# One product for q, k and v per token tile, keys normalised before the transpose, biases inside shifted weights

## The chip, the core and the metric

The kernel runs on one core of a Trainium2 chip. The metric is the device time of a run in microseconds (us). Of the kernel before there are three runs; their median is 128.02 us, the lowest 126.82 us, the highest 130.88 us. TensorE (PE), VectorE (DVE), ScalarE (ACT) and GpSimd (POOL) each work through a queue of their own in order; the DMAs here are issued on the queues of SyncE (SP) and ACT.

## The reference, cut to what matters

The input x is 4 batches of 512 tokens with 128 channels. A context of 4 x 77 tokens with 96 channels comes with a mask. Two blocks are computed, each added to its input:

```
ln = layernorm(layernorm(x)) * gl + bl        # latents, 128 channels
xn = layernorm(ctx) * gx + bx                 # context, 96 channels
q  = ln @ Wq.T;  k, v = [xn @ Wkv.T ; ln @ Wlkv.T]      # 77 + 512 keys, 2 heads of 64
qn = rmsnorm(q) * gq / 8;  kn = rmsnorm(k) * gk          # per head
out = softmax(qn @ kn.T, masked context keys) @ v
x  = x + out @ Wo.T + bo
h  = layernorm(x);  gates = softmax(h @ Wg + bg)          # 8 experts
x  = x + sum over the 2 largest gates of  gate * (h @ W[e] + b[e])
```

All eight expert products are computed for every token, and the gates that are not chosen are zero.

## The kernel before

Tokens are handled in tiles of 128 (T = 4 per batch, 16 in all). `FRONT` lists the units of the first part (batch 0 in two units of two tiles, the others whole), `REAR` those of the rest (batch 3 in two halves). Four strings, `TENSOR` (L27), `VECTOR` (L48), `SCALAR` (L61) and `GPSIMD` (L72), write out by hand in which order each engine issues its jobs; each word names a function of that engine, a unit and an index. In `TENSOR` the last word of a job names its PSUM banks, and `free` (L937) makes PE wait until the bank's former user has been read. Between engines all is ordered by semaphores.

The front of a unit: DVE takes the statistics (`stats1`), POOL the inverse root with a power (`rstd1`), DVE normalises (`apply1`), PE transposes (`xT`, L985), ACT applies gain and bias (`lnT`, L513). PE then makes q token-major (`q`, L994: lnT loaded, 128 columns of Wq streamed), v likewise (`v`, L1012), and k channel-major (`k`, L1003: the weight loaded, up to 512 tokens streamed). q is squared (ACT), summed (DVE `ssq`), raised to -0.5 (POOL `rq`, L395), multiplied (DVE `qn`) and transposed (`qT`). k is squared on ACT and summed over channels by small products with `heads` (`ssk`, L1022); its inverse root `rk` (POOL, L401) is not applied to k: it is the scale of the exponential (L588), whose partitions are the keys. Queries and keys are each split into a rounded part and a rest (`QH`, `QL`, `KH`, `KL`), and a score is three products of float32r parts (L1077).

The attention: for each batch and each of 5 blocks of keys (4 of 128 tokens, 1 of 77 context tokens) PE makes the scores of both heads, ACT takes one exponential per head, PE multiplies with v (`value`, L1098). For the denominators POOL adds key blocks 0+1 and 2+3 (`e01` L420, `e23` L429), DVE adds the two sums and the context block (`esum1` L796, `esum2` L803), and PE sums over partitions (`den`, L1111), followed by a transpose (`denT`), the output projection (`proj`, L1132) and the sum with x (`xbo`, `x2`).

The experts: second normalisation (`stats2`, `rstd2`, `apply2` L843), transpose (`l2T`, L1141), two copies on ACT and a rest on POOL (`l2L`, L457), gate logits token-major (`gate`, L1150: 32 loads of tokens with 8 columns each), the two best gates (`logits`, `top`), a transpose of split gates and one product with a block matrix of biases (`w3`, `gateT`, `wT`, `bias` L1167, `x2b`). For each tile experts 0 to 3 (`low`) and 4 to 7 (`high`) are each three products of 512 columns (L945 to L947). ACT scales the four low experts (L635), POOL adds them (`pair` L470, L471), DVE adds the high ones in a chain (`high`, L923, for two tiles at a time), POOL makes the last sum (`res`, L479), and SP stores. In `TENSOR` four `high` blocks of batch 0 stand among the scores of batches 2 and 3, and one `low` block in batch 3's.

## Time and profile before

| what | value |
|---|---|
| median of 3 runs | 128.02 us (126.82 to 130.88) |
| profiled execution: span from first to last instruction | 123.7 us |
| profiled execution's own time beside its span | not listed apart; the median run is 4.3 us over the span, the lowest 3.1 us |
| mean granted TensorE clock | 0.958 of full |
| PE busy (matmuls) | 106.9 us, 86% |
| DVE busy | 97.5 us, 79% |
| POOL busy | 91.0 us, 74% |
| ACT busy | 76.6 us, 62% |
| last instruction's end to the end of the span | 121.6 to 123.7 us: the last store |

The span is the time between the first and the last instruction of one profiled execution. Busy time is a sum over the whole span. The ends of matmuls are modelled, since they are pipelined; what one costs in a full queue is read from the distance between two starts. A group such as "x8" holds eight instructions of one kind in a row. A product of plain float32 operands shows as two instructions, one of float32r operands as one.

### The profile page before, as it was taken

The page shows a single profiled execution, that of the slowest core. Times are in us where ns is not written, and L with a number is a line of the kernel's source. Part 1 is how long each engine was busy: PE and PEld are TensorE (multiplying, and loading weights), DVE is VectorE, ACT ScalarE, POOL GpSimd, SP SyncE. Part 2 cuts the span into 40 slices and gives each one's busy share as a digit, 9 for nine tenths or more (in the row PEclk, how much of TensorE's full clock was granted, in tenths as well). Part 3 has the DMA queues.
Part 4 walks back from the last instruction along what each step waited for, and adds up shares of the span by engine and source line. Part 5 has one row for each costly group of instructions (what it writes and reads, how often), then busy time and mean ns, then how long its engine had stood idle before and what let it go on. Part 6 is the DMA issues. An engine that isn't in the chain of part 4 may idle for free. (4 is left out here: it accounts for less than half of the span.)

```text
span 123.7 us, 2493 instructions
## 1 busy us (share of the span) xinstructions
PE 106.9 (86%) x683; PEld 69.0 (56%) x683; DVE 97.5 (79%) x376; ACT 76.6 (62%) x177; POOL 91.0 (74%) x117
## 2 busy tenths in 40 slices
...
GB/s 122 119 22 130 168 169 0 5 0 0 0 3 0 5 0 0 0 0 5 0 5 0 0 0 5 0 0 5 0 42 3 3 42 42 38 10 42 42 42 42
DMA packets 5971, 3.44 MB, mean 28 GB/s; under 512 B 2407, under 2 KB 5575, under 8 KB 5959
## 3 DMA queue, kind: packets, MB, share of 16 engines
...
q10 hardware_dynamic: 832, 0.36, 1.1%
...
q14 instruction: 6, 0.05, 0.1%
HBM read 2.24 MB, written 1.05 MB: 27 GB/s over the span
## 5 line engine op out<-in xcount | busy, mean ns | idle before, releaser
L588 ACT ACTIVATE probs<-PS,shift,rk 128x512 f32<-128x512 f32 (+1 forms) x40 | 25.5, 691 | 9.6 <-PE PS L1077 9.3
L635 ACT ACTIVATE scaled<-PS,w 128x128 f32<-128x128 f32 x64 | 18.4, 375 | 9.7 <-PE PS L947 7.0
L1098 PE MATMUL PS<-probs,V_sb 128*64 128x512 f32 (+1 forms) x80 | 18.2, 532 | 0.0
L420 POOL TENSOR_TENSOR esum<-probs,probs 128x1024 f32<-128x1024 f32 (+1 forms) x5 | 10.7, 2147 | 7.2 <-ACT probs L588 7.2
L945 PE MATMUL PS<-WeH,l2H 128*128 128x512 f32 x32 | 14.3, 446 | 0.5 <-ACT scaled L635 0.5
L470 POOL TENSOR_TENSOR pair<-scaled 128x256 f32<-128x256 f32 x16 | 12.0, 751 | 2.8 <-ACT scaled L635 1.5
L946 PE MATMUL PS<-WeL,l2H 128*128 128x512 f32 x32 | 13.3, 414 | 0.0
L947 PE MATMUL PS<-WeH,l2L 128*128 128x512 f32 x32 | 13.1, 410 | 0.0
L429 POOL TENSOR_TENSOR e<-probs,probs 128x1024 f32<-128x1024 f32 (+1 forms) x5 | 9.7, 1936 | 2.6 <-ACT probs L588 2.6
L1077 PE MATMUL PS<-QH,KH 64*128 64x512 f32 (+1 forms) x40 | 9.5, 463 | 0.4 <-DVE QL L766 0.4
L719 DVE TENSOR_SCALAR xh<-x_sb,mv,rstd 128x128 f32<-128x128 f32 x16 | 8.1, 566 | 2.0 <-POOL rstd L388 2.0
L923 DVE SCALAR_TENSOR_TENSOR part<-PS,w,part 128x128 f32<-128x128 f32 x32 | 8.9, 340 | 0.0
L1077 PEld LDWEIGHTS PS<-QH,KH 64*128 64x128 f32 x40 | 4.2, 198 | 8.4 <-issue 7.2
L843 DVE TENSOR_SCALAR l<-x,mv,rstd 128x128 f32<-128x128 f32 x16 | 7.8, 542 | 1.1 <-POOL rstd L448 1.1
L471 POOL TENSOR_TENSOR low<-pair 128x128 f32<-128x128 f32 x16 | 7.7, 482 | 1.3
L945 PEld LDWEIGHTS PS<-WeH,l2H 128*128 128x128 f32 x32 | 6.4, 200 | 3.2 <-issue 1.1
L479 POOL TENSOR_TENSOR x2b<-low,acc 128x128 f32<-128x128 f32 x16 | 7.3, 462 | 0.9 <-DVE acc L923 0.7
L591 ACT ACTIVATE probs<-PS,cbias,crk 77x512 f32<-77x512 f32 (+1 forms) x10 | 6.4, 686 | 2.6 <-PE PS L1077 1.8
L1077 PE MATMUL PS<-QL,KH 64*128 64x512 f32 (+1 forms) x40 | 7.9, 381 | 0.0
L457 POOL TENSOR_TENSOR l2L<-l2T,l2H 128x512 fp32r<-128x512 f32 (+1 forms) x5 | 5.3, 1059 | 3.3 <-ACT l2H L618 3.3
L1077 PE MATMUL PS<-QH,KL 64*128 64x512 f32 (+1 forms) x40 | 7.8, 375 | 0.0
L401 POOL TENSOR_TENSOR rk<-msk,half 128x8 f32<-128x8 f32 (+1 forms) x5 | 7.1, 1424 | 0.9 <-DVE msk L743 0.9
...
## 6 DMA issues: line engine op xcount, KB each, us to landing
out_dram<-x2b SPq DMA_DIRECT2D x7, 128.0 KB, 1.7
...
x_sb<-in_x_dram SPq DMA_DIRECT2D x2, 128.0 KB, 2.4
bias_raw<-in_L_ffn_b_dram SPq DMA_DIRECT2D x12, 4.0 KB
Wlkv_sb<-in_L_xattn_Wlkv_dram ACTq DMA_DIRECT2D x1, 128.0 KB, 2.8
...
```

The lines of the kernel that those rows point to most:

```text
L420: pool.tensor_tensor(esum[p % 2][:, :, s], probs[p % 2][0][:, :, s], probs[p % 2][1][:, :, s], ALU.add).then_inc(e01_made, 1)
L429: pool.tensor_tensor(e23[:, :, s], probs[p % 2][2][:, :, s], probs[p % 2][3][:, :, s], ALU.add).then_inc(e23_made, 1)
L470: step(pool.tensor_tensor(pair[:], scaled[m % 2][:, 0:EH // 2], scaled[m % 2][:, EH // 2:EH], ALU.add))
L588: act.activation(probs[p % 2][n][:, h, s], ps[:, s], ACT.Exp, bias=shift[:, 0:1], scale=rk[:, b, n, h:h + 1]).then_inc(probs_made, 1)
L635: last = act.activation(scaled[m % 2][:, e], ps[:, e], ACT.Copy, scale=w[:, m, e:e + 1])
L719: last = dve.tensor_scalar(xh[:, b % 2, t], x_sb[:, b, t], mv1[:, b, t, 0:1], rstd1[:, b, t:t + 1], ALU.subtract, ALU.mult)
L923: last = dve.scalar_tensor_tensor(dst, bank("high", p, 2 * n + k)[:, e * C:(e + 1) * C], w[:, m, EH + e:EH + e + 1], src, ALU.mult, ALU.add)
L945: pe.matmul(dst, lH, rH, start=True, stop=False)
L946: pe.matmul(dst, lH, rL, start=False, stop=False)
L947: return pe.matmul(dst, lL, rH, start=False, stop=True)
L1077: last = pe.matmul(bank("score", p, n, h)[0:P if n < T else M, 0:(e - a) * P], k, queries[r, b % 2, a * P:e * P], start=(step == 0), stop= ...
L1098: last = pe.matmul(bank("value", p, 0)[h * D:(h + 1) * D, s], v, pr, start=(n == 0), stop=(n == KT - 1))
```

## The change

All front units have two tiles, the rear units are whole batches. PE makes q, k and v of a tile in one product of 384 columns into two adjacent banks (`qkv`; PSUM is now four tensors of two banks). Keys are treated as queries are: squares, sums, power and product token-major over 256 channels (`sq`, `ssq`, `rq`, `qkn`), then both are transposed (`qkT`) and split (`qkH`, `qkL`). The context is handled alike (`ckv`, `csq`, `ctx_ss`, `ckn`, `ckT`). The exponential has no per-key scale any more and covers both heads in one instruction over two banks. DVE's two sums for the denominators are gone; PE sums three sources instead (`den`). A normalised row sums to zero, so the last channel's weight can be subtracted from all others and the last row and channel used for the bias: expert and gate weights are shifted on POOL (`weS`, `wgS`), channel 127 of `l2` is one, and the bias product with its preparation is gone. The expert weights are split on ACT (`weH`) and POOL (`weL`) rather than on DVE, and loaded after all of x. The gate is computed channel-major: 32 weight columns loaded, 128 tokens streamed, the four tiles in four groups of columns, for both parts of the tokens; ACT copies, and PE transposes. The rest `l2L` moves from POOL to DVE and reads PSUM. POOL's last sums go over two tiles at once. All four orders are written anew; 31 of the 32 expert blocks now stand behind the last `value` (before, 27).

```diff
-FRONT = ((0, 0, 2), (0, 2, 4), (1, 0, 4), (2, 0, 4), (3, 0, 4))
-REAR = ((0, 0, 4), (1, 0, 4), (2, 0, 4), (3, 0, 2), (3, 2, 4))
-
+FRONT = tuple((b, a, a + 2) for b in range(4) for a in (0, 2))
+REAR = ((0, 0, 4), (1, 0, 4), (2, 0, 4), (3, 0, 4))
+JOINED = (0, 1, 2, 3)
...
+    weights 0 0 0   weights2 0 0 1   xT 0 0 0   xT 1 0 2   qkv 0 0 45   ctxT 0 0 0   qkv 1 0 23   xT 3 0 0   ckv 0 0 67
+    qkv 3 0 01   qkT 0 0 4   xT 2 0 5   qkT 1 0 2   maskT 0 0 3   qkv 2 0 45   ckT 0 0 3   score 0 0 67   score 0 1 01
+    score 0 2 23   qkT 3 0 6   value 0 0 7   score 0 3 01   value 0 1 -   score 0 4 23   value 0 2 -   xT 4 0 0
+    xT 7 0 1   value 0 3 -   xT 5 0 1   value 0 4 -   qkT 2 0 0   qkv 4 0 23   qkv 5 0 45   score 1 3 01   xT 6 0 6
+    den 0 0 7   score 1 0 01   proj 0 0 67   score 1 1 23   denT 0 0 0   value 1 0 1   score 1 2 45   value 1 1 -
+    score 1 4 23   value 1 2 -   qkT 5 0 0   value 1 3 -   qkT 4 0 2   value 1 4 -   qkv 6 0 45   score 2 3 01
+    score 2 0 23   den 1 0 6   qkv 7 0 01   score 2 1 67   score 2 2 23   qkT 6 0 4   value 2 0 5   score 2 4 67
+    value 2 1 -   l2T 0 0 4   qkT 7 0 0   proj 1 0 12   value 2 2 -   denT 1 0 3   gate 0 0 0   value 2 3 -
+    score 3 0 67   value 2 4 -   score 3 3 01   den 2 0 4   proj 2 0 52   score 3 1 67   denT 2 0 3   value 3 0 4
+    score 3 2 01   l2T 1 0 6   gateT 0 0 7   value 3 1 -   score 3 4 23   value 3 2 -   gate 1 0 5   value 3 3 -
+    gateT 1 0 5   low 0 3 6   value 3 4 -   den 3 0 7   proj 3 0 01   denT 3 0 7   high 0 0 2   low 0 2 3   high 0 1 6
+    low 0 0 4   low 0 1 5   high 0 2 3   high 0 3 7   l2T 2 0 4   low 1 3 2   low 1 2 5   gate 2 0 4   low 1 1 2
+    gateT 2 0 4   low 1 0 6   high 1 3 3   high 1 1 5   high 1 2 7   high 1 0 6   l2T 3 0 2   low 2 2 4   gate 3 0 7
+    low 2 3 0   low 2 1 1   gateT 3 0 4   low 2 0 7   high 2 1 5   high 2 2 0   high 2 3 6   high 2 0 4   low 3 2 7
...
+    consts 0 0   stats1 0 0   stats1 1 0   ctx_stats 0 0   apply1 0 0   apply1 1 0   gain 0 0   mask 0 0   stats1 3 0
+    ctx_apply 0 0   stats1 2 0   apply1 3 0   ssq 0 0   shift 0 0   ssq 1 0   apply1 2 0   qkn 0 0   ctx_ss 0 0
+    qkn 1 0   ssq 3 0   qkL 0 0   ckn 0 0   cbias 0 0   qkL 1 0   qkn 3 0   ckL 0 0   stats1 6 0   stats1 7 0
+    stats1 4 0   ssq 2 0   stats1 5 0   apply1 7 0   apply1 6 0   apply1 4 0   apply1 5 0   qkn 2 0   qkL 3 0   qkL 2 0
+    ssq 4 0   ssq 5 0   qkn 4 0   qkn 5 0   x2 0 0   qkL 5 0   qkL 4 0   stats2 0 0   ssq 6 0   apply2 0 0   qkn 6 0
+    ssq 7 0   qkL 6 0   qkn 7 0   l2L 0 0   qkL 7 0   x2 1 0   stats2 1 0   apply2 1 0   x2 2 0   logits 0 0   l2L 1 0
+    stats2 2 0   mark 0 0   logits 1 0   top 0 0   mark 1 0   apply2 2 0   top 1 0   x2 3 0   sum 0 0   stats2 3 0
+    l2L 2 0   sum 0 1   logits 2 0   apply2 3 0   mark 2 0   sum 1 1   l2L 3 0   top 2 0   sum 1 0   logits 3 0
+    mark 3 0   top 3 0   sum 2 1   sum 2 0   sum 3 1   sum 3 0
 """
...
+    ident 0 0   rstd1 0 0   blanks 0 0   rstd1 1 0   ctx_rstd 0 0   rstd1 3 0   rstd1 2 0   rq 0 0   rq 1 0   ctx_rk 0 0
+    rq 3 0   xbo 1 0   xbo 0 0   rstd1 6 0   rstd1 7 0   rstd1 4 0   rstd1 5 0   rq 2 0   e01 0 0   e23 0 0   rq 4 0
+    rq 5 0   weS 0 0   e01 1 0   e23 1 0   xbo 2 0   wgS 0 0   rstd2 0 0   rq 6 0   rq 7 0   e01 2 0   e23 2 0
+    rstd2 1 0   weL 0 0   e01 3 0   e23 3 0   rstd2 2 0   xbo 3 0   pair 0 1   pair 0 0   rstd2 3 0   res 0 0   res 0 1
+    pair 1 1   pair 1 0   res 1 1   pair 2 1   res 1 0   pair 2 0   res 2 1   pair 3 1   res 2 0   res 3 1   pair 3 0
+    res 3 0
...
+        PS = [st.enter_context(nc.psum_tensor(f"PS{n}", [P, 2, S], F32)) for n in range(4)]
...
+            sp.wait_ge(Wg_zeroed, 2)
+            sp.dma_start(WgS[P - 1:P, 0:E], row(bg)).then_inc(bg_in, 16)
+            sp.dma_start(We_sb[0:P - 1], We[:, 0:P - 1].rearrange("e h o -> h e o")).then_inc(We_in, 16)
+            sp.dma_start(We_last[:], We[:, P - 1:P].rearrange("e h o -> h e o").to_broadcast([P - 1, E, C])).then_inc(We_in, 16)
+            sp.dma_start(We_sb[P - 1:P], be.rearrange("(a e) o -> a e o", a=1)).then_inc(We_in, 16)
...
+            def weS_(p, n):
+
+                pool.wait_ge(We_in, 48)
+                pool.tensor_tensor(We_sb[0:P - 1], We_sb[0:P - 1], We_last[:], ALU.subtract).then_inc(WeS_made, 1)
+
+            def weL_(p, n):
+
+                pool.wait_ge(WeH_made, 1)
+                pool.tensor_tensor(WeL[:], We_sb[:], WeH[:].bitcast(F32), ALU.subtract).then_inc(WeL_made, 1)
+
+            def wgS_(p, n):
+
+                pool.wait_ge(Wg_in, 32)
+                pool.tensor_tensor(WgS[0:P - 1, 0:E], Wg_sb[:], Wg_last[:], ALU.subtract).then_inc(WgS_made, 1)
+
...
+            def sq_(p, n):
+                b, a, e = FRONT[p]
+                act.wait_ge(qkv_done, after("pe", "qkv", p))
+                if p >= 2:
+                    act.wait_ge(ssq_made, after("dve", "ssq", p - 2))
+                act.activation(qksq[:, p % 2], both("qkv", p, 0)[:, :, 0:2 * C], ACT.Square).then_inc(qksq_made, 1)
+
+            def v_(p, n):
+                b, a, e = FRONT[p]
+                act.wait_ge(qkv_done, after("pe", "qkv", p))
...
+            def qkH_(p, n):
+
+                b, a, e = FRONT[p]
+                act.wait_ge(qkT_done, after("pe", "qkT", p))
                 act.wait_ge(gain_made, 1)
...
+                    act.wait_ge(scores_done, after_all("pe", "score", [(b - 2, k) for k in range(KT)]))
+                act.activation(QH[:, b % 2, a * P:e * P], bank("qkT", p, 0)[:, 0:(e - a) * P], ACT.Copy, scale=gain[:, 0:1])
+                act.copy(KH[:, b % 2, a * P:e * P], bank("qkT", p, 0)[:, (e - a) * P:2 * (e - a) * P]).then_inc(qkH_made, 1)
...
+                ps = both("score", p, n)
+                    act.activation(probs[p % 2][n][:], ps[:], ACT.Exp, bias=shift[:, 0:1], scale=1.0).then_inc(probs_made, 1)
+                    act.activation(probs[p % 2][n][0:M], ps[0:M], ACT.Exp, bias=cbias[:, p:p + 1],
+                                   scale=1.0).then_inc(probs_made, 1)
...
+            def gs_(p, n):
+                b, a, e = REAR[p]
+                act.wait_ge(gate_done, after("pe", "gate", p))
+                act.copy(gsb[0:(e - a) * GW, p], bank("gate", p, 0)[0:(e - a) * GW, 0:P]).then_inc(gs_made, 1)
...
+            def qkn_(p, n):
+                b, a, e = FRONT[p]
+                dve.wait_ge(rqk_made, after("pool", "rq", p))
+                dve.wait_ge(v_made, after("act", "v", p))
+                if p >= 2:
+                    dve.wait_ge(qkT_done, after("pe", "qkT", p - 2))
+                dve.tensor_tensor(qkn[:, p % 2].rearrange("p t (g d) -> p t g d", d=D),
+                                  both("qkv", p, 0)[:, :, 0:2 * C].rearrange("p t (g d) -> p t g d", d=D),
+                                  rqk[:, b, a:e].unsqueeze(3).to_broadcast([P, e - a, 2 * H, D]),
+                                  ALU.mult).then_inc(qkn_made, 1)
...
+                dve.wait_ge(qkH_made, after("act", "qkH", p))
...
+                dve.scalar_tensor_tensor(QL[:, b % 2, a * P:e * P], bank("qkT", p, 0)[:, 0:g], gain[:, 0:1],
+                                         QH[:, b % 2, a * P:e * P].bitcast(F32), ALU.mult, ALU.subtract)
+                dve.tensor_tensor(KL[:, b % 2, a * P:e * P], bank("qkT", p, 0)[:, g:2 * g],
+                                  KH[:, b % 2, a * P:e * P].bitcast(F32), ALU.subtract).then_inc(qkL_made, 1)
...
-            def esum1_(p, n):
-
-                s = slice(0, (REAR[p][2] - REAR[p][1]) * P)
-                dve.wait_ge(e01_made, p + 1)
-                dve.wait_ge(e23_made, p + 1)
-                step(dve.tensor_tensor(esum[p % 2][:, :, s], esum[p % 2][:, :, s], e23[:, :, s], ALU.add))
-
-            def esum2_(p, n):
-
-                s = slice(0, (REAR[p][2] - REAR[p][1]) * P)
-                dve.wait_ge(dve_step, count[0])
-                dve.wait_ge(probs_made, H * KT * (p + 1))
-                dve.tensor_tensor(esum[p % 2][0:M, :, s], esum[p % 2][0:M, :, s], probs[p % 2][T][0:M, :, s],
-                                  ALU.add).then_inc(esum_made, 1)
...
+                    last = dve.tensor_scalar(l2[:, b % 2, t, 0:C - 1], x2[:, b, t, 0:C - 1], mv2[:, b, t, 0:1],
+                                             rstd2[:, b, t:t + 1], ALU.subtract, ALU.mult)
...
+            def l2L_(p, n):
+                b, a, e = REAR[p]
+                dve.wait_ge(l2H_made, after("act", "l2H", p))
+                dve.tensor_tensor(l2L[:, b % 2, a * P:e * P], bank("l2T", p, 0)[:, 0:(e - a) * P],
+                                  l2H[:, b % 2, a * P:e * P].bitcast(F32), ALU.subtract).then_inc(l2L_made, 1)
...
+                    last = pe.matmul(both("qkv", p, 0)[:, t - a, 0:3 * C], lnT[:, b % 2, t * P:(t + 1) * P], WT[:],
+                                     start=True, stop=True)
+                last.then_inc(qkv_done, 1)
...
+            def qkT_(p, n):
+                b, a, e = FRONT[p]
+                free("qkT", p, 0)
+                pe.wait_ge(qkn_made, after("dve", "qkn", p))
+                for s in range(2):
+                    for t in range(a, e):
+                        k = s * (e - a) + t - a
+                        last = pe.transpose(bank("qkT", p, 0)[:, k * P:(k + 1) * P], qkn[:, p % 2, t - a, s * C:(s + 1) * C], ident[:])
+                last.then_inc(qkT_done, 1)
...
+                sources = [(e01[k], P), (e23, P), (probs[k][T], M)] if p in JOINED else \
+                    [(e01[k], P), (probs[k][2], P), (probs[k][3], P), (probs[k][T], M)]
+                pe.wait_ge(e01_made, after("pool", "e01", p))
+                if p in JOINED:
+                    pe.wait_ge(e23_made, after("pool", "e23", p))
+                pe.wait_ge(probs_made, after_all("act", "exp", [(p, i) for i in range(KT)]))
+                for i, (src, rows) in enumerate(sources):
+                    for h in range(H):
+                        for g in range(2):
+                            r = slice((2 * h + g) * 32, (2 * h + g + 1) * 32)
+                            last = pe.matmul(bank("den", p, 0)[r, 0:c], ones[0:rows], src[0:rows, h, g * c:(g + 1) * c],
+                                             start=(i == 0), stop=(i == len(sources) - 1))
                 last.then_inc(den_done, 1)
...
+                pe.wait_ge(bg_in, 16)
+                for i, tokens in enumerate((l2H, l2L)):
+                    for t in range(a, e):
+                        last = pe.matmul(bank("gate", p, 0)[(t - a) * GW:(t - a + 1) * GW, 0:P], WgS[:],
+                                         tokens[:, b % 2, t * P:(t + 1) * P].bitcast(F32), start=(i == 0), stop=(i == 1))
```

## Rows read from the trace of the kernel before

**Rows 1.** Windows; columns: PE, PEld, DVE, ACT, POOL busy (count); PEclk; DMA; GB/s.

```profile
17.50:86.60 69.10, 68.66 (x488) 39.32 (x488) 57.71 (x189) 47.92 (x86) 50.14 (x39) 0.98 0.01 2
86.60:123.70 37.10, 27.33 (x133) 20.83 (x131) 29.31 (x136) 20.21 (x71) 30.65 (x55) 0.91 0.09 29
```

**Rows 2.** Timeline of PE, 46 to 57 us: start, duration, what.

```profile
46.59 1.02 PE L1003 MATMUL PS<-lnT,WT 128*128 128x512 f32 x2
...
50.41 0.50 PE L1077 MATMUL PS<-QH,KH 64*128 64x512 f32 x2
...
51.31 1.08 PE L1098 MATMUL PS<-probs,V_sb 128*64 128x512 f32 x4
52.31 1.05 PE L1022 MATMUL PS<-heads,ksq 128*128 128x2 f32 x8
53.23 0.63 PE L1141 MATMUL PS<-ident,l 128*128 128x128 f32 x4
...
54.80 0.64 PE L1111 MATMUL PS<-esum,ones 128*32 128x256 f32 x8
55.37 1.06 PE L1150 MATMUL PS<-Wg_sb,l2T 128*128 128x8 f32 x8
56.28 0.41 PE L1120 MATMUL PS<-ident,den_sb 128*128 128x128 f32 x2
```

**Rows 3.** Timeline of PE at 256 columns, and the last value product.

```profile
78.15 0.39 PE L1077 MATMUL PS<-QH,KH 64*128 64x256 f32 x2
...
78.69 0.65 PE L1098 MATMUL PS<-probs,V_sb 128*64 128x256 f32 x4
...
86.04 0.65 PE L1098 MATMUL PS<-probs,cV 77*64 77x256 f32 x4
```

**Rows 4.** Timeline of PE in the tail: two expert blocks of three products.

```profile
91.68 0.39 PE L945 MATMUL PS<-WeH,l2H 128*128 128x512 f32 x1
...
92.38 0.40 PE L945 MATMUL PS<-WeH,l2H 128*128 128x512 f32 x1
```

**Rows 5.** Timeline of the head, all engines.

```profile
10.94 0.58 ACT L513 ACTIVATE lnT<-PS,ln_cols 128x256 f32<-128x256 f32 x1
...
17.52 0.61 PE L1077 MATMUL PS<-QH,KH 64*128 64x512 f32 x2 [0.36 <-DVE QL L766]
```

**Rows 6.** Groups with shapes kept apart: the power and the exponential.

```profile
L588 ACT ACTIVATE probs<-PS,shift,rk 128x512 f32<-128x512 f32 x24 | 17.3, 776 | 7.6 <-PE PS L1077 7.5
...
L588 ACT ACTIVATE probs<-PS,shift,rk 128x256 f32<-128x256 f32 x16 | 8.2, 565 | 2.0 <-PE PS L1077 1.7
...
L395 POOL TENSOR_TENSOR rq<-msq,half 128x8 f32<-128x8 f32 x3 | 5.0, 1660 | 0.2
```

**Rows 7.** Windows of 2 us where the granted clock fell, columns as rows 1.

```profile
18.00:20.00 2.00, 2.00 (x12) 1.84 (x10) 1.97 (x13) 0.95 (x2) 2.00 (x3) 0.50 0.00 1
...
110.00:112.00 2.00, 2.00 (x6) 1.52 (x6) 1.90 (x14) 0.22 (x1) 1.75 (x4) 0.50 0.00 0
```

**Rows 8.** Groups by line: out<-in xcount, busy, mean ns, idle before.

```profile
L923 DVE SCALAR_TENSOR_TENSOR part<-PS,w,part 128x128 f32<-128x128 f32 x32 | 8.9, 340 | 0.0
...
L401 POOL TENSOR_TENSOR rk<-msk,half 128x8 f32<-128x8 f32 (+1 forms) x5 | 7.1, 1424 | 0.9 <-DVE msk L743 0.9
...
L796 DVE TENSOR_TENSOR esum<-esum,e 128x1024 f32<-128x1024 f32 (+1 forms) x5 | 6.0, 1193 | 0.9 <-POOL e L429 0.9
L803 DVE TENSOR_TENSOR esum<-esum,probs 77x1024 f32<-77x1024 f32 (+1 forms) x5 | 5.4, 1083 | 0.0
```

**Rows 9.** Timeline of POOL in the tail.

```profile
112.32 0.73 POOL L470 TENSOR_TENSOR pair<-scaled 128x256 f32<-128x256 f32 x1 [0.17 <-POOL x2b L479]
...
114.18 0.75 POOL L470 TENSOR_TENSOR pair<-scaled 128x256 f32<-128x256 f32 x1 [0.17 <-POOL x2b L479]
```

**Rows 10.** Timeline of DVE: the second normalisation, twice.

```profile
51.20 1.12 DVE L843 TENSOR_SCALAR l<-x,mv,rstd 128x128 f32<-128x128 f32 x4 [0.91 <-POOL rstd L448]
...
65.45 2.71 DVE L843 TENSOR_SCALAR l<-x,mv,rstd 128x128 f32<-128x128 f32 x4
```

More of the change, by code:

```diff
@@ L484, in _ @@
+            for kind, p, n in JOBS["pool"]:
+                does[kind](p, n)
         @block.scalar
@@ new lines, in dens_, with oT_ @@
+            def dens_(p, n):
+                act.wait_ge(den_done, after("pe", "den", p))
+                if p >= 2:
+                    act.wait_ge(denT_done, after("pe", "denT", p - 2))
+                act.copy(den_sb[:, p % 2], bank("den", p, 0)[:, 0:S // 2]).then_inc(dens_made, 1)
+            def oT_(p, n):
+                act.wait_ge(values_done, after("pe", "value", p, KT - 1))
+                if p >= 2:
+                    act.wait_ge(proj_done, after_all("pe", "proj", rears(p - 2)))
+                act.copy(oT[:, p % 2], bank("value", p, 0)[:]).then_inc(oT_made, 1)
@@ L641, in _ @@
+            for kind, p, n in JOBS["act"]:
+                does[kind](p, n)
         @block.vector
@@ L817, in x2_ @@
+                dve.wait_ge(denT_done, after("pe", "denT", b))
+                c = T // 2
+                sums = bank("denT", b, 0)[:, 0:c * P].rearrange("p (c h g k) -> p c h g k", c=c, h=H, g=2)
+                for g in range(a // c, e // c):
+                    divided = step(dve.reciprocal(rden[:, b, g * c:(g + 1) * c], sums[:, :, :, g, 0]))
+                dve.wait_ge(proj_done, after("pe", "proj", p))
                 dve.wait_ge(dve_step, divided)
@@ new lines, in sum_ @@
+                        if e < EH - 1:
+                            summed[i] = step(last)
+                last.then_inc(acc_made, 1)
+            does = dict(consts=consts_, gain=gain_, shift=shift_, mask=mask_, cbias=cbias_, stats1=stats1_,
+                        apply1=apply1_, ssq=ssq_, qkn=qkn_, qkL=qkL_, ctx_stats=ctx_stats_, ctx_apply=ctx_apply_, ctx_ss=ctx_ss_,
+                        ckn=ckn_, ckL=ckL_, x2=x2_, stats2=stats2_, apply2=apply2_, l2L=l2L_, logits=logits_, mark=mark_,
+                        top=top_, sum=sum_)
@@ L935, in _ @@
+            for kind, p, n in JOBS["dve"]:
+                does[kind](p, n)
         @block.tensor
@@ L1146, in gate_ @@
                 free("gate", p, 0)
[L1147 to L1151 removed]
+                pe.wait_ge(l2L_made, after("dve", "l2L", p))
+                pe.wait_ge(WgS_made, 1)
+                pe.wait_ge(Wg_zeroed, 2)
+                pe.wait_ge(bg_in, 16)
```

868 lines of the change are left out of this document (319 added, 549 removed).

## The prediction

> **What bounds the kernel now.** I read the totals on the page first: PE 86%, DVE 79%, POOL 74% and ACT 62% busy. No engine is full over the whole span, so I cut the span where its limit changes, and asked for each engine's busy time in each piece. The cuts are the first score at 17.5 us [rows 5] and the end of the last product of probabilities with values [rows 3]. That gives a head of 17.5 us, an attention part of 69.1 us and a tail of 37.1 us, 123.7 in all.
>
> In the attention part PE is busy 68.7 of 69.1 us, DVE 57.7, POOL 50.1, ACT 47.9 [rows 1]. The reader is to see that only PE has no room: a microsecond taken from another engine there is worth nothing by itself. In the tail PE has 27.3 of 37.1 us, DVE 29.3 and POOL 30.7 [rows 1], and 2.5 us at the very end are the last store with what goes before it. There POOL works tile after tile at 1.86 us [rows 9], and DVE is nearly as full. The head is a chain of single steps, each waiting for the one before: from the second unit's `lnT` to the first score it takes 6.6 us [rows 5].
>
> PE's costs I take from the distance between two starts in the full stretch [rows 2], since busy times of pipelined products overlap. Where a group's successor is not shown I take its busy time less 0.07 us, by which the value product's 1.08 exceeds its distance of 1.00.
>
> **The head: +2.5 us.** In the chain to the first score, k now goes every way that q goes. The product is 384 columns wide where q was 128: two products of 512 columns take 0.95 us [rows 2], so 4 x 256 added columns take 0.95. The power on POOL is 128x8 and takes 1.66 us [rows 6]; the narrow form is (7.1 - 3 x 1.66) / 2 = 1.06 [rows 6, 8], so +0.6. Square, sum, product, rounding and rest are each 256 elements wider, and by the exponential's 0.72 against 0.51 us of busy time each such step costs 0.2 [rows 6]: +1.0. Sum 2.55. Against it, PE makes `xT` of both units before any product, and for it, `ctx_stats` now stands ahead of `apply1` on DVE. Bounds: 0 (a chain that runs wholly inside waits that are there already) to +4.5 (each of the two units pays most of it, since POOL's powers queue). I take 2.5.
>
> **The attention part: -6.5 us**, all on PE.
> - `xT` and `qkv` of batch 1 move into the head, where PE has holes: four transposes 0.56, and 8 x 384 columns at 0.475 per 512, 2.85 [rows 2]. Together -3.4. What hides them is PE's wait for the first keys; without that cover they come back in full.
> - q, k and v stream as many columns as before, 3 x 1,024 per batch: 0 (at best -0.3 for fewer switches).
> - `ssk` goes, 0.92 per batch [rows 2], batches 1 to 3: -2.8. The transposes of k come, 0.56 each: +1.7.
> - The denominators have three sources: 0.57 becomes 1.71 [rows 2] in three batches: +3.4. This is the price of DVE's sums, 6.0 + 5.4 us [rows 8], which lay beside PE's work. `den` now waits for POOL's `e23` itself. The worst place is batch 3, where `proj` and nearly all experts are queued behind `den` on PE; between the exponential that `e23` needs and `den` lie three value products, a score, a gate and an expert block, over 5 us, against POOL's one sum.
> - The gate: 0.91 us now [rows 2]. Sixteen products of 128 columns in four column groups cost 0.57 if they run as `den` does (eight of 256 columns, 0.57), and 1.8 if the groups do not overlap at 0.11 each. The former is the nearer row, also in four groups: -0.3 in two batches, -0.6.
> - Batch 3 is no longer halved: ten scores at 0.54 and ten values at 0.58 [rows 3] become five at 0.90 and five at 1.00 [rows 2]: 11.2 - 9.5, -1.7.
> - Expert blocks in this part fall from 5 to 1, 0.70 each [rows 4]: -2.8, which the tail takes over. One bias product: -0.25.
>
> The sum is -6.45. ACT's gain, 16 x 2 exponentials into 16, is several us, but ACT was idle 21 us here; 0. POOL loses `rk`, 7.1 us [rows 8], and `l2L`, and gets eight wide powers and two passes over the expert weights; it stays far under PE. SP's queue issues fewer DMAs (twelve small bias loads go), and x comes before the expert weights. Those, with a spread copy of their last row about twice the bytes, are first waited for by POOL behind its sixth `rq`, well inside this part; queued there is `e01` of batch 1, on which only its `den` waits: 0.
>
> **The tail: -2 us.** PE: 31 blocks at 0.70 are 21.7; `den` 1.7, `proj` and `denT` 1.2, two `l2T` 1.1, two gates with transposes 1.5, so 27.2. After the last block come DVE's sums of two tiles, 8 x 0.28 = 2.2 [rows 8], POOL's last sum and the store, 3.6: 33.0 if PE sets the pace. POOL per two tiles needed 3.72 [rows 9]; wider instructions bring it between 1.86 (only fixed cost) and 3.72 (none), I take the middle near 2.9, 23 for eight, and `l2L` is off it. So POOL stops being the limit. DVE is next: it must wait for the third part of `x2`, about 5.6 us into the tail, then do eight pairs, 17.8, and second statistics, normalisation, `l2L`, two or three rounds of gates, about 8: 31.4, and 3.6 to the end, 35. DVE sets the end, at 35 against 37.1. Bounds: 33 and 38.
>
> **Sum.** +2.5 - 6.5 - 2 = -6, so the span goes from 123.7 to 117.7. The median of the runs shown is 4.3 us over the span; I carry that along: 128.0 - 6 = **122 us**.
>
> **Rivals.** A difference of 2% is about what a measurement of this kernel can tell from none: 125.5 and 130.6 us are the marks.
> - *Nothing is waited for more, and the clock stays up.* The granted clock was 0.50, that is 1.2 GHz, in 18 to 20 us, after PE had waited in the head, and again in 110 to 112, after holes in the tail [rows 7]; each window lost 1 us. If the head stays at 17.5 and half of these losses go, and DVE keeps up with PE in the tail: 122 - 2.5 - 2 - 1 = 116.5. For: all four engines get less work. Against: the longer chain. Chance 0.18.
> - *The saving is waited away at both ends.* The head at its upper bound (+2) and DVE at 37 in the tail (+2): 126. For: DVE's order mixes sums with gates, and the `high` banks are freed only by them. Chance 0.17.
> - *POOL's longer instructions hold DVE.* The second normalisation takes 1.12 us alone, but 2.71 when POOL is inside a sum [rows 10]. In the tail it stands twice beside POOL sums twice as wide as now: 2 x 1.6, 125.2. Chance 0.06. [...]
> - *Slower: each batch starts with a wait.* The first score of a batch now needs the keys and queries of both its units, by `after_all`, and the chain before it is 6.6 + 2.5 us long. In batches 1 to 3 PE has work for it only if the hand-written orders place the units early enough on four engines. If PE waits 2.5 us at each and then works 2 us at half clock, as after the head [rows 7], that is 2.5 + 1 in each, 10.5 in all: 132.5. It decides from 2.9 us a batch (8.6 to the mark). For: there are eight powers of 1.66 on POOL. Against: DVE and POOL had 11 and 19 us to spare in the attention part. Chance 0.13. The Trainium skill, "TensorE: Matmul & The Clock Gate", section "What's actually happening", says that the slow clock is the default and activity releases it; that speaks against a change that takes work off PE and lengthens its first wait.
>
> My forecast has 0.46. Faster by over 2%: 0.46 + 0.18 + 0.05 of the lock's 0.06 = 0.69. Within 2%: 0.17 + 0.01 = 0.18. Slower: 0.13. The range runs from 115 (the best case and 1.5 us of its unknowns) to 129 (the second rival and 3 us); the last rival is left out, and a little at the lower end.
>
> **What would show it.** First score near 20 us. The part from there to the last value product near 62.5 us with PE busy throughout; each `den` near 1.7 us between starts, a `qkv` unit near 1.4, a gate near 0.6. In the tail DVE the fullest engine and POOL at 3 us or less per two tiles. I am wrong if PE has holes ahead of the first score of batches 1 to 3, if `den` waits for POOL, or if POOL still sets the end.

## Result: 11% slower, and the profile after

The changed kernel takes 141.65 us (median of 4 runs, 141.38 to 141.81) beside 128.06 us for the kernel before (126.82 to 130.88) on the same chip: a ratio of 1.114, 95% interval 1.105 to 1.123. The forecast was 122, range 115 to 129. The profiled run took 141.38 us with a span of 139.6, so 1.8 us lie around a span. The runs of one kernel fall into two groups (the kernel before near 126 and near 131); every ratio here compares lower group with lower group, so it isn't the quotient of the medians, and below I give the median of a kernel's lower group beside that of all its runs, as "lower median".

Page of the changed kernel: the span in 40 slices, 3.5 us each.

```profile
span 139.6 us, 2250 instructions
...
PE   0587987999999995000089999999999996799940
...
PEclk9999999999999999755558999999999999559999
DMA  4354000000000000000000000000000020101121
GB/s 133 80 123 143 17 22 24 22 27 22 24 22 22 27 22 22 22 21 2 0 0 0 0 5 0 0 2 0 5 0 0 5 78 0 38 2 38 38 75 38
```

Two things are new. PE, which had no hole in this part before [rows 1], stands empty in slices 17 to 20. And a transfer runs at 22 GB/s for fourteen slices, from about 14 to 63 us, where none ran before: the attention part had 2 GB/s [rows 1]. The same as windows; columns are those of rows 1:

```profile
14.00:34.00 20.00, 18.72 (x96) 9.80 (x94) 14.77 (x48) 13.72 (x26) 17.18 (x20) 1.00 0.08 22
...
70.00:80.00 10.00, 9.75 (x58) 4.38 (x58) 3.90 (x9) 5.77 (x9) 7.87 (x9) 0.78 0.00 0
```

The reader is to see the DMA share of 0.08: 0.08 x 16 = 1.3, so about one of the 16 DMA engines was at work for 20 us. Timeline of SP's queue in the changed kernel, which says what it moved (start, duration of the issue, what):

```profile
12.95 0.26 SPq L354 DMA_DIRECT2D We_sb<-in_L_ffn_W_dram  x1
13.25 22.60 SPq L355 DMA_DIRECT2D We_last<-in_L_ffn_W_dram  x1
35.89 23.85 SPq L356 DMA_DIRECT2D We_sb<-in_L_ffn_b_dram  x1
```

The two wide loads cover 127 partitions, since the last row of each expert's weights was split off. The issue *behind* each takes 22.6 and 23.9 us instead of 0.3 to 0.6 (e1 below). 127 x 1024 elements of 4 bytes are 520 KB; in 23 us that is 22.6 GB/s. Timelines of POOL and then PE in the changed kernel, with the idle time ahead of an instruction in brackets (the instruction before on POOL ends at 41.77):

```profile
63.07 2.34 POOL L423 TENSOR_TENSOR We_sb<-We_sb,We_last 127x1024 f32<-127x1024 f32 x1 [21.30 <-DMA We_sb<-in_L_ffn_b_dram]
65.37 2.34 POOL L440 TENSOR_TENSOR e<-probs,probs 128x1024 f32<-128x1024 f32 x1
67.66 2.34 POOL L447 TENSOR_TENSOR e<-probs,probs 128x1024 f32<-128x1024 f32 x1
```
```profile
70.25 1.93 PE L1018 MATMUL PS<-e,ones 128*32 128x256 f32 x16 [16.09 <-POOL e L447]
```

POOL reaches `weS` at 41.8 us and stands 21.3 us. Behind it are `e01` and `e23` of batch 1, behind them `den` 1, and on PE everything stands behind `den` 1: 16.1 us idle, and half clock afterwards (0.78 of full in the window 70 to 80, so about 2.2 us more, an estimate). Together 18.3 us. The attention part of this kernel, from its first score at 23.7 us to its last value product, takes 76.9 us, that of the next kernel 58.8: the stall explains this difference of 18.1 us.

```profile
23.70:100.60 76.90, 60.81 (x421) 28.18 (x419) 36.35 (x138) 37.87 (x59) 44.96 (x39) 0.89 0.04 12
```

Head (23.7 us) and tail (39.0 us) are longer than before too, by 6.2 and 1.9 us; e1 and what follows it is about them.

### The profile page after: what moved, and what is told of

The parts are those of the page before. It is cut to its first block, busy times and chain, and to the rows that moved or that the text cites. A ratio compares the mean times of both kernels' runs of the same rounds, so it can differ in the third digit from the quotient of the medians.

```text
span 139.6 us, 2250 instructions
## 1 busy us (share of the span) xinstructions
PE 108.0 (77%) x651; PEld 60.1 (43%) x651; DVE 82.4 (59%) x334; ACT 68.0 (49%) x153; POOL 81.7 (59%) x92
## 3 DMA queue, kind: packets, MB, share of 16 engines
HBM read 2.71 MB, written 1.05 MB: 27 GB/s over the span
## 4 chain that ended last, share of the span: by engine, by line
PE 46%; issue 21%; DVE 12%; POOL 9%; SPq 5%; ACT 3%; DMA 2%; POOLq 1%; DVEq 0%; ACTq 0%
PE PS L999 11%; PE PS L981 8%; PE PS L933 6%; PE PS L1018 4%; DVE part L871 3%; POOL rqk L406 2%; PE PS L1039 2%; PE PS L1082 2%; DVE l L804 2%; PE PS L1083 2%; PE PS L1084 2%; POOL pair L473 2%; POOL e L440 2%; SPq L340 2%; POOL e L447 2%
## 5 line engine op out<-in xcount | busy, mean ns | idle before, releaser
L804 DVE TENSOR_SCALAR l<-x,mv,rstd 128x127 f32<-128x127 f32 x16 | 8.5, 593 | 20.3 <-POOL rstd L460 20.3
L586 ACT ACTIVATE probs<-PS,shift 128x1024 f32<-128x1024 f32 x16 | 17.6, 1116 | 4.9 <-PE PS L981 4.2
L473 POOL TENSOR_TENSOR pair<-scaled 128x512 f32<-128x512 f32 x8 | 10.3, 1287 | 12.6 <-ACT scaled L636 12.3
L1018 PE MATMUL PS<-e,ones 128*32 128x256 f32 x64 | 5.1, 447 | 16.1 <-POOL e L447 16.1
L999 PE MATMUL PS<-probs,V_sb 128*64 128x512 f32 x64 | 17.3, 618 | 0.0
L933 PE MATMUL PS<-WT,lnT 128*128 128x384 f32 x32 | 15.3, 615 | 1.1 <-ACT lnT L515 0.9
L423 POOL TENSOR_TENSOR We_sb<-We_sb,We_last 127x1024 f32<-127x1024 f32 x1 | 2.3, 2340 | 21.3 <-DMA We_sb<-in_L_ffn_b_dram 21.3
L406 POOL TENSOR_TENSOR rqk<-msq,half 128x8 f32<-128x8 f32 x8 | 13.3, 1658 | 0.7
L440 POOL TENSOR_TENSOR e<-probs,probs 128x1024 f32<-128x1024 f32 x4 | 9.5, 2364 | 1.1 <-ACT probs L586 1.1
L933 PEld LDWEIGHTS PS<-WT,lnT 128*128 128x128 f32 x32 | 7.0, 237 | 6.6 <-issue 3.4
L447 POOL TENSOR_TENSOR e<-probs,probs 128x1024 f32<-128x1024 f32 x4 | 9.4, 2357 | 0.0
L716 DVE TENSOR_TENSOR qkn<-PS,rqk 128x512 f32<-128x512 f32 x8 | 5.5, 689 | 4.9 <-POOL rqk L406 4.8
## 6 DMA issues: line engine op xcount, KB each, us to landing
out_dram<-x SPq DMA_DIRECT2D x8, 128.0 KB, 1.7
x_sb<-in_x_dram SPq DMA_DIRECT2D x2, 128.0 KB, 2.5
Wlkv_sb<-in_L_xattn_Wlkv_dram ACTq DMA_DIRECT2D x1, 128.0 KB, 2.9
```

Source lines behind the costliest of these rows:

```text
L406: pool.tensor_tensor(rqk[:, b, a:e], msq[:, b, a:e], half[:, 0:2 * H * (e - a)].rearrange("p (t h) -> p t h", h=2 * H), ALU.pow).then_inc( ...
L440: pool.tensor_tensor(e01[p % 2][:], probs[p % 2][0][:], probs[p % 2][1][:], ALU.add).then_inc(e01_made, 1)
L473: step(pool.tensor_tensor(pair[:], s[:, :, 0:EH // 2], s[:, :, EH // 2:EH], ALU.add))
L586: act.activation(probs[p % 2][n][:], ps[:], ACT.Exp, bias=shift[:, 0:1], scale=1.0).then_inc(probs_made, 1)
L933: last = pe.matmul(both("qkv", p, 0)[:, t - a, 0:3 * C], lnT[:, b % 2, t * P:(t + 1) * P], WT[:], start=True, stop=True)
L999: last = pe.matmul(bank("value", p, 0)[h * D:(h + 1) * D, :], v, pr, start=(n == 0), stop=(n == KT - 1))
```

## The experiments

My theory (A): a load over 127 partitions runs on one DMA engine, and holds the queue that issued it; the rest of the change saves what was forecast. Rivals: (A') it is the spreading read, the size or anything short of a whole 128; (B) the stall is POOL's order alone, or something else in the change is slow.

**e1_loads_128.** Both wide loads over 128 partitions; the biases then overwrite row 127, and SP waits for the loads before it issues them.

```diff
-            sp.dma_start(We_sb[0:P - 1], We[:, 0:P - 1]...).then_inc(We_in, 16)
-            sp.dma_start(We_last[:], We[:, P - 1:P]....to_broadcast([P - 1, E, C])).then_inc(We_in, 16)
+            sp.dma_start(We_sb[:], We...).then_inc(We_in, 16)
+            sp.dma_start(We_last[:], We[:, P - 1:P]....to_broadcast([P, E, C])).then_inc(We_in, 16)
+            sp.wait_ge(We_in, 32)
```

> The changed kernel with both loads of expert weights (the weights and the spread copy of their last row) over 128 partitions instead of 127, and the bias row stored over row 127 once they have landed; nothing else differs. Theory A, the 127 partitions put each load on one DMA engine: the loads land before 25 us, POOL's subtraction of the last row waits for nothing (21.3 us now), the window 55 to 70 us is full of PE work, and the time falls by 16 to 22 us to 120 to 126 us, so under the kernel before. Theory B, the loads are late because they are 1 MB and stand behind x in the queue, whatever their partitions: landing still near 63 us, time still 141. Theory C, the changed kernel is slow for its longer chains and the wait only sits on a slack: the wait goes, the time falls by less than 5 us.

Measured: 121.13 us (119.35 to 123.08), lower median 119.8, ratio 0.949, interval 0.941 to 0.958. One partition more in two loads is worth about 21 us (ratio 0.949 for 1.114). Timeline of SP:

```profile
12.96 0.40 SPq L354 DMA_DIRECT2D We_sb<-in_L_ffn_W_dram  x1
13.41 0.58 SPq L355 DMA_DIRECT2D We_last<-in_L_ffn_W_dram  x1
```

Windows of head, attention part and tail, columns as rows 1, cut at this kernel's first score and last value product (the profile is of its longest run, 123.08 us):

```profile
0.00:24.50 24.50, 15.99 (x55) 9.28 (x55) 14.45 (x59) 9.66 (x21) 14.40 (x28) 1.00 0.42 112
24.50:83.30 58.80, 58.80 (x421) 27.35 (x419) 36.44 (x139) 37.93 (x59) 45.11 (x39) 1.00 0.01 2
83.30:121.30 38.00, 29.82 (x179) 21.68 (x177) 31.49 (x139) 20.50 (x73) 23.13 (x26) 0.93 0.08 28
```

The attention part has no hole in 58.8 us, so nothing of rival B is left there. The head is still 7.0 us longer than before and the tail of this run 0.9.

**e2_shift_late.** The slow loads stay; `weS` moves behind the sums of batch 2 in POOL's order.

```diff
-    rq 5 0   weS 0 0   e01 1 0   e23 1 0 ... e01 2 0   e23 2 0
+    rq 5 0   e01 1 0   e23 1 0 ... e01 2 0   e23 2 0   weS 0 0
```

> The changed kernel with its slow loads kept; only POOL's subtraction of the last weight row stands later in POOL's order, behind the sums e01 and e23 of batch 2 instead of before those of batch 1. Theory A with the queueing as the damage (POOL in order, behind it e01 and e23 of batch 1, den of batch 1 on PE waits for them): the loads still land near 63 us, but POOL no longer waits 21 us there; time 121 to 129 us. If the loads themselves disturbed the other engines (B), the time stays above 138 us.

Measured: 122.87 us (120.58 to 123.88), lower median 120.6. The queue is as slow as ever, `We_last` 22.28 and the biases 23.85 us, but POOL now has its sums done first:

```profile
64.61 2.36 POOL L447 TENSOR_TENSOR e<-probs,probs 128x1024 f32<-128x1024 f32 x1
66.93 2.37 POOL L423 TENSOR_TENSOR We_sb<-We_sb,We_last 127x1024 f32<-127x1024 f32 x1
```

So the load is harmful only through what stands in order behind the one who waits for it. Both halves are needed: a slow load, and a wait placed ahead of sums that PE needs.

**e3_before_127.** The kernel before with only its expert load cut into 127 and 1 partitions.

```diff
-            sp.dma_start(We_sb[:], We...).then_inc(We_in, 16)
+            sp.dma_start(We_sb[0:P - 1], We[:, 0:P - 1]...).then_inc(We_in, 16)
+            sp.dma_start(We_sb[P - 1:P], We[:, P - 1:P]...).then_inc(We_in, 16)
```

> The kernel BEFORE with one edit: its load of the expert weights goes as 127 partitions plus one instead of 128. Theory A: the load of 508 KB lands near 33 us instead of near 15 us, so DVE waits some 12 to 15 us in its weight split at 20 us and the time rises by 8 to 14 us to 136 to 142. Theory B (bytes and place in the queue decide): the same bytes at the same place, time unchanged at 128 within 1%.

Measured: 147.8 us (147.64 to 148.08), ratio 1.172, interval 1.164 to 1.179: even more than expected. Timeline of SP, then the longest waits on DVE and on PE (total, times, longest):

```profile
10.08 25.37 SPq L341 DMA_DIRECT2D We_sb<-in_L_ffn_W_dram  x1
...
39.72 0.82 SPq L348 DMA_DIRECT2D x_sb<-in_x_dram  x2
```
```profile
DVE stat L708 <- DMA x_sb<-in_x_dram: 22.3, 2, 20.3
...
PE PS L995 <- DVE cms L789: 15.0, 1, 15.0
```

I had priced the late expert weights. What cost the time was the queue: the x of batches 2 and 3, issued behind, left SP at 39.7 us. DVE stood 20.3 us for it and PE 15.0 us behind DVE, and when DVE came to the weights at 44.0 us it didn't wait for them.

**e4_loads_126.** Each of the two loads as 126 partitions and 1.

```diff
+            for r in (slice(0, P - 2), slice(P - 2, P - 1)):
+                sp.dma_start(We_sb[r], We[:, r]...).then_inc(We_in, 16)
+                sp.dma_start(We_last[r], ....to_broadcast([n, E, C])).then_inc(We_in, 16)
```

> The changed kernel with each of the two loads cut into 126 partitions and 1 partition. Theory A in the form that a load uses the largest number of engines up to 16 that divides its partition count: 126 gives 14 engines, so the loads land before 27 us and the time is that of the 128-partition variant within 2 us. Theory A', that only multiples of 16 partitions are spread over the engines: the loads stay near 22 GB/s and the time at 141.

Measured: 122.65 us (two runs, 120.91 and 124.40), so a lower median of 120.9. The issue behind the first wide load takes 0.56 us, where it took 22.6, and the page shows 227 GB/s in the slice that had 22:

```profile
13.60 0.33 SPq L356 DMA_DIRECT2D We_sb<-in_L_ffn_W_dram  x1
13.97 0.56 SPq L357 DMA_DIRECT2D We_last<-in_L_ffn_W_dram  x1
```

So it is not the missing 128th partition, it is the number 127. The Trainium skill, "DMA: Bandwidth & Descriptors", section "Why a DMA increments its semaphore by 16 and not by 1", states that a copy is spread over the largest number of engines up to 16 that divides the slowest dimension (of those with more than one element) of both its sides, and names 127 partitions as a case for one engine. By that rule 126 gets 14. The traces agree at all three sizes tried as to one engine or many (share 0.08 for 127, over 200 GB/s for 126 and 128); that it is 14 no run here shows.

**e7_one_slow_load.** Half the dose: `We_sb` stays over 127 partitions, `We_last` goes over 128.

```diff
-            sp.dma_start(We_last[:], We[:, P - 1:P]....to_broadcast([P - 1, E, C])).then_inc(We_in, 16)
+            sp.dma_start(We_last[:], We[:, P - 1:P]....to_broadcast([P, E, C])).then_inc(We_in, 16)
```

> The changed kernel with `We_sb` still loaded over 127 partitions and only the spread copy of the last row over 128. Theory that a 508 KB load over 127 partitions occupies about 23 us by itself: the biases' issue no longer takes 23.8 us, the loads have landed by 38 to 42 us, before `weS` is reached at 41.8, and the time is 121 to 123, nearly all of the 20 us back. Rival, that only the order of both together or the spreading read makes it slow: We_last's issue still takes over 20 us and the time is over 130.

Measured: 121.66 us (120.44 and 122.88), so a lower median of 120.4. Timelines of SP and of POOL at `weS`:

```profile
13.79 22.49 SPq L355 DMA_DIRECT2D We_last<-in_L_ffn_W_dram  x1
36.33 1.50 SPq L356 DMA_DIRECT2D We_sb<-in_L_ffn_b_dram  x1
```
```profile
43.37 2.38 POOL L423 TENSOR_TENSOR We_sb<-We_sb,We_last 127x1024 f32<-127x1024 f32 x1 [0.80 <-DMA We_sb<-in_L_ffn_b_dram]
```

The loads are in by 43.4 us, a little later than expected, and POOL waits 0.8 us for them at `weS`. One such load was all but free; the second cost about 20 us.

**e5_head_order.** From here on the base is e1, and the question is why its head is 24.5 us where 20 was forecast. `ctx_apply` moves ahead of `stats1` 3 on DVE, `mask` behind `shift`.

```diff
-    gain 0 0   mask 0 0   stats1 3 0   ctx_apply 0 0   stats1 2 0   apply1 3 0   ssq 0 0   shift 0 0   ssq 1 0
+    gain 0 0   ctx_apply 0 0   stats1 3 0   stats1 2 0   apply1 3 0   ssq 0 0   shift 0 0   mask 0 0   ssq 1 0
```

> The changed kernel with both wide loads over 128 partitions (as in e1_loads_128), and on DVE `ctx_apply` ahead of `stats1` 3 and `mask` behind `shift`, so that DVE no longer stands 3.17 us for the mask's load at 8.0 us. Theory that this wait, and ctxT behind it, makes a part of the head's +7.0 us: ctxT comes right behind qkv 0 (11.8 instead of 13.1), qkv 1 1.3 us earlier, first score 22.5 to 23.2 instead of 24.5, time 119.5 to 120.0 beside 121.1. Rival, that the head is long because of PE at half clock and POOL's powers alone: first score 24 or later, time as e1.

Measured: 119.14 us (118.38 to 121.63), ratio 0.945, interval 0.936 to 0.953. Timelines of e1: DVE's wait, and what it held on PE.

```profile
11.16 0.19 DVE L675 CAST maskf<-mask 4x77 f32<-4x77 uint8 x1 [3.17 <-DMA mask<-in_mask_BxS_bk_dram]
```
```profile
13.10 0.72 PE L953 MATMUL PS<-ident,cxh 77*96 77x77 f32 x4 [1.31 <-DVE cxh L746]
```

The same products in e5, and its first score:

```profile
8.64 2.93 PE L934 MATMUL PS<-WT,lnT 128*128 128x384 f32 x4
...
11.88 2.44 PE L934 MATMUL PS<-WT,lnT 128*128 128x384 f32 x4
...
22.00 0.50 PE L982 MATMUL PS<-QH,KH 64*128 64x512 f32 x2
```

The first score comes 2.5 us earlier than in e1, of the 7.0 by which the head had grown. The other traces bear this out: 24.4 us in e6, which has the old order, 22.0 in e10 and 21.3 in e9, which have the new one. In time the gain isn't shown by this run alone: the lower median falls from 119.8 to 118.7, but the intervals of the two ratios overlap.

**e6_pool_yields.** As e1, but POOL waits with its first `res` until DVE has done `apply2` 3.

```diff
             def res_(p, n):
+                if (p, n) == (0, 0):
+                    pool.wait_ge(l2_made, after("dve", "apply2", 3))
```

> As e1_loads_128, but POOL waits with its first `res` until DVE has finished `apply2` 3. In e1 the four instructions of that `apply2` took 3.17 us beside POOL's `res` and `pair` sums where 1.11 is the time alone, and PE stood 1.75 us at gate 3 and went to half clock at 102 to 106 us. Theory that POOL's sums hold the DVE instruction: `apply2` 3 takes 1.1 us, the tail loses 2 to 3 us, 118 to 119. Rival, that the tail is bound by DVE's own work elsewhere or by POOL: 1.1 us too, but the time stays at 121 or rises, as POOL starts 1.7 us later.

Measured: 119.68 us (118.93 to 120.50), ratio 0.951, interval 0.942 to 0.960. The lower median is 119.7 too, and that of e1 was 119.8. Timelines of DVE, POOL and PE in e1: `apply2` 3, the sums beside it, and the gate behind.

```profile
95.52 3.17 DVE L805 TENSOR_SCALAR l<-x,mv,rstd 128x127 f32<-128x127 f32 x4
```
```profile
94.89 1.43 POOL L482 TENSOR_TENSOR x<-low,acc 128x256 f32<-128x256 f32 x2
96.49 1.32 POOL L474 TENSOR_TENSOR pair<-scaled 128x512 f32<-128x512 f32 x1 [0.17 <-POOL x L482]
```
```profile
102.25 0.54 PE L1063 MATMUL PS<-l2H,WgS 128*32 128x128 f32 x8 [1.75 <-DVE acc L872]
```

Of e6, `apply2` 3 and the small product `w` on DVE, and POOL in the tail:

```profile
95.42 1.11 DVE L807 TENSOR_SCALAR l<-x,mv,rstd 128x127 f32<-128x127 f32 x4
...
100.67 1.09 DVE L853 TENSOR_TENSOR w<-ew,erc 128x32 f32<-128x32 f32 x1
```
```profile
104.27 1.32 POOL L474 TENSOR_TENSOR pair<-scaled 128x512 f32<-128x512 f32 x1 [1.05 <-ACT scaled L639]
...
107.28 1.29 POOL L474 TENSOR_TENSOR pair<-scaled 128x512 f32<-128x512 f32 x1 [0.17 <-POOL x L484]
```

The normalisation takes 1.11 instead of 3.17 us, as the theory has it: POOL's sums did hold it. In these two traces the tail, from the end of the last value product, is 35.4 us instead of 38.0, and it now ends with POOL, at 107.28 - 104.27 = 3.01 us per two tiles. But that is one run against the longest run of e1, in which the clock also fell to 0.54 at 104 to 106 us, after the gate's wait; and the expected 118 to 119 us didn't come. By the lower medians (119.7 and 119.8) the time stayed, which is what the rival said. A part of the reason stands in the trace: POOL's sums, moved back, now hold `w` (1.09 and 0.69 us in the tail, 0.19 both times in e1). ACT's `scaled` waits 2.62 us behind the first of them, and POOL's `pair` at 104.27 waits 1.05 for ACT.

**e8_all_three.** e5 and e6 with three moves more: on PE `ckv` ahead of `xT` 3 and `qkT` 0 ahead of `qkv` 3, and on DVE `l2L` 3 ahead of `sum` 1 1.

```diff
-    xT 3 0 0   ckv 0 0 67   qkv 3 0 01   qkT 0 0 4   xT 2 0 5   qkT 1 0 2   maskT 0 0 3   qkv 2 0 45
+    ckv 0 0 67   xT 3 0 0   qkT 0 0 4   qkv 3 0 01   qkT 1 0 2   maskT 0 0 3   xT 2 0 5   qkv 2 0 45
-    mark 2 0   sum 1 1   l2L 3 0   top 2 0
+    mark 2 0   l2L 3 0   sum 1 1   top 2 0
```

> e5 and e6 together, with `ckv` ahead of `xT` 3 and `qkT` 0 ahead of `qkv` 3 on PE, and `l2L` 3 ahead of `sum` 1 1 on DVE. If the gains add: first score 21.5 to 22, tail 2 to 3 us shorter, 115.5 to 117. If the head's gain is only moved into a wait inside attention, 118.

Measured: 123.40 us (122.81 to 123.53), ratio 0.979, interval 0.973 to 0.986; the expectation failed by 6 us. Timeline of PE:

```profile
17.96 0.63 PE L947 MATMUL PS<-ident,qkn 128*128 128x128 f32 x4 [1.81 <-DVE qkn L719]
...
22.59 1.99 PE L936 MATMUL PS<-WT,lnT 128*128 128x384 f32 x4 [1.75 <-ACT lnT L518]
...
25.03 0.80 PE L984 MATMUL PS<-QH,KH 64*128 64x512 f32 x2
```

`qkv` 3 had filled exactly the time in which `qkn` 0 is made. Moved behind, PE waits at `qkT` 0 and again at `qkv` 2, and the first score starts at 25.0 instead of 22.0, and takes 0.80 us for 0.50. In the tail gate 3 waits 2.77 us for a bank that `sum` 1 1 frees, where it had waited 1.13 in e6.

**e9_two_orders.** e5 and e6 without those moves; its edit is the two diffs shown there.

> The DVE order of e5_head_order and the POOL wait of e6_pool_yields together, with none of the other moves of e8_all_three. If the two gains are separate ones: 121.1 - 2.0 - 1.4 = 117.7, first score 22.0 us, `apply2` 3 at 1.1 us, tail 35.4. This says too whether e8's 123.4 came from its moves on PE (`qkT` 0 ahead of `qkv` 3, PE waiting 1.8 us there and again before `qkv` 2) and of `l2L` 3: then 117 to 118.5 here; if the two orders disturb each other it stays over 120.

Measured: 118.30 us (117.42 to 118.85), ratio 0.939, interval 0.933 to 0.945. The two orders don't disturb each other, and e8's loss of 5.1 us against this came from its other moves; which of them, no run separates. The 2.0 and 1.4 us in the expectation were differences between medians of all runs. By the lower medians the two orders together gain 119.8 - 118.3 = 1.5 us over e1; 1.1 of it is there with e5's order alone (118.7), and the rest is within the noise. Windows of e9, attention part and tail:

```profile
21.30:80.15 58.85, 58.85 (x421) 27.35 (x419) 36.54 (x139) 37.87 (x59) 45.19 (x39) 1.00 0.01 2
80.15:115.60 35.45, 28.15 (x179) 20.63 (x177) 29.83 (x139) 20.33 (x73) 23.00 (x26) 0.99 0.09 31
```

**e10_tail_order.** e9 with `apply2` 3 ahead of `logits` 2, and `low` 2 3 ahead of `gate` 3.

```diff
-    logits 2 0   apply2 3 0
+    apply2 3 0   logits 2 0
-    low 2 2 4   gate 3 0 7   low 2 3 0
+    low 2 2 4   low 2 3 0   gate 3 0 7
```

> e9 with `apply2` 3 ahead of `logits` 2 on DVE, so that POOL is released 0.6 us earlier, and with expert block `low` 2 3 ahead of `gate` 3 on PE, in the 1.13 us in which the gate waits for its bank. Theory that POOL's sums end the tail (in e6 they follow each other from 104 us on): 0.6 us less than e9, 117.1. Rival, that DVE's sums end it: no change, or 0.3 more, since `logits` 2 come later.

Measured: 118.58 us (117.19 to 119.05), lower median 118.4, ratio 0.938, interval 0.928 to 0.948: not to be told from e9. No change is what the rival said, though the trace gives another reason than DVE's sums: POOL's last row of pairs starts no earlier, since ACT's `scaled` are late now (POOL waits 1.86 us for them at 102.1, 1.05 in e9). In the traces of e6 and e9 POOL's sums do end the tail, but an earlier start for them is worth nothing while their feeder is late.

**e11_warm_pe.** e10 with 17 transposes of the identity, read by nobody, in PE's first two waits.

```diff
+            def warm_(p, n):
+                for _ in range((11, 6)[p]):
+                    pe.transpose(PS[3][:, 1, 0:P], ident[:], ident[:])
```

> e10 with 11 transposes of the identity into an unused bank while PE waits for the first weights, and 6 more while it waits for the first `xT`; nothing reads them. In e5 the two first `qkv` products took 2.93 and 2.44 us where 1.46 is the time at full clock. Theory that PE's idle start is why they run at half speed, and that this lengthens the head: `qkv` 0 at 1.5 us, first score 20.0 to 20.8 instead of 22.0, time 1.2 to 2 us below e10. Rival, that the chain over ACT, DVE and POOL and the loads set the head: the products are faster, the first score stays at 21.5 to 22.

Measured: 118.68 us (117.01 to 120.24), lower median 118.6, ratio 0.939, interval 0.930 to 0.949. Timeline of PE in its longest run:

```profile
8.81 1.95 PE L941 MATMUL PS<-WT,lnT 128*128 128x384 f32 x4
...
10.86 1.50 PE L941 MATMUL PS<-WT,lnT 128*128 128x384 f32 x4
...
17.80 0.63 PE L952 MATMUL PS<-ident,qkn 128*128 128x128 f32 x4 [1.23 <-DVE qkn L719]
19.02 2.13 PE L941 MATMUL PS<-WT,lnT 128*128 128x384 f32 x4 [0.44 <-DVE KL L733]
...
21.59 0.79 PE L989 MATMUL PS<-QH,KH 64*128 64x512 f32 x2
```

The second product is at full speed (1.50 us for 2.10 in e10), and the first score comes at 21.6 for 22.0, inside the rival's range; the time is as e10's. PE reaches `qkT` 0 1.6 us earlier than in e10, but then waits 1.2 us at `qkT` 1 for DVE's `qkn`, which leaves 0.8. So the chain over POOL, DVE and ACT takes back about half of the gain. In this run the granted clock also fell, to 0.50 in 20 to 22 us, and from 19.0 us to the first score PE took 2.6 us for what took 1.7 in e10. How early the score comes when the clock stays up, this run doesn't show.

## Why the prediction was wrong

**The step that failed** is in its attention part: "SP's queue issues fewer DMAs ... Those, with a spread copy of their last row about twice the bytes, are first waited for by POOL behind its sixth `rq`, well inside this part; queued there is `e01` of batch 1, on which only its `den` waits: 0." I counted DMAs and bytes and took the rate of the kernel before for granted; I didn't ask what the new shape does to it. That 0 was about 21 us by e1: a wait of 21.3 us on POOL, of which 16.1 arrived on PE. The names behind the wait were right, but I wrote "only its `den`", though PE works in order and nothing passes a `den`. None of the four rivals had a load in it: the sum of chances left nothing for what happened. My slower rival had waits at the start of each batch as mechanism, for POOL's powers among others; in e1 PE has no hole in the attention part at all. Of my signs of being wrong, `den` waiting for POOL is the one that came.

**The rest of the sum.** Without that one number the forecast stands: e1 gives 121.1 (lower median 119.8), e9 118.3, beside 122. By terms that is partly luck, as the errors of the parts cancel in part: head +4.5, attention -3.8 and tail +2.9 us against the forecast in the trace of e1.
- *Head:* forecast +2.5 with bounds of 0 and 4.5; +7.0 in e1, +4.5 in e5, +3.8 in e9. 2.5 of it is DVE's place for `mask` and `ctx_apply`, by the first score of e5. I had noted `ctx_stats` ahead of `apply1`, but not looked for DMAs among the moved steps. The product itself was mis-sized too: `qkv` 0 takes 2.93 us where the same product takes 1.46 from 16 us on; I had priced the added columns at the full-speed rate. e11 made the second one fast and gained no time by it.
- *Attention:* forecast -6.5, to 62.5 us; measured 58.8, so -10.3, in e1 and e9 alike. `den` takes 40.99 - 39.55 = 1.44 in e1 instead of 1.71, 0.8 in three batches: two sources of 128 rows in a row take 0.89 (39.55 to 40.44), less than twice the 0.57 that I took from one alone, and the 77-row source 0.55. No half clock at its start and no idle: 1.0 and 0.4 [rows 7, 1]. `proj` has 48 instructions for 56, 0.3. The q, k and v of batches 2 and 3 take 2.68 and 2.98 us where they took 2.84 each: 0. The remaining 1.3 us I can't place.
- *Tail:* forecast -2, to 35 us, DVE at the end; +0.9 in e1, then 35.4 in e6 and e9. My estimate of POOL, 2.9 us per two tiles (the middle of my bounds was 2.79), was measured at 3.0. But in e6 and e9 it is POOL that ends the tail, not DVE; the size came out right for another reason.
- *The lock:* I gave the rival "POOL's longer instructions hold DVE" a chance of 0.06 and 2 x 1.6 us. The mechanism is there: e1 shows it once in the tail, at 3.17 - 1.11 = 2.06 us, and e6 shows that it goes when POOL waits. Its price in time isn't shown, since e6 is no faster than e1. A second such place, in the attention part (3.15 us at 68.7 in e9), is hidden: PE has no idle time there.
- *The gate* takes 0.57 us (66.34 to 66.91 in e1) as forecast, and the expert blocks moved as counted.

**From span to median.** I carried 4.3 us. The runs here have 1.8 us around each span, so my span of 117.7 should have been read as 119.5; e1's lower median is 119.8 and e9's 118.3. The 4.3 us came from setting the span of a run near 125.5 beside the median of 128.0.

What is shown in time: the loads (e1, e3, e4, e7) and the order behind them (e2). What is shown in traces only: the effect of DVE's order on the first score (e5, e9, e10) and the hold on `apply2` (e6). What is only argued: the terms of the attention part, read off the trace; no part of the change but the shape of the load (e3) was put alone into the kernel before.
